# A routed matrix product with a convolution ahead of it: x gathers moved ahead, last expert choice and one block load put earlier

## The reference

```python
y = conv_general_dilated(x, cond_2048[:, None, :], ..., feature_group_count=D) + b   # 8 taps, causal
logits = einsum('bsh,eh->bse', y, w_router);  idx = argmax(logits, axis=-1)
out = x + take_along_axis(einsum('bsh,efh->bsef', y, w_experts), idx)                # one of 8 experts
```

## Time and profile before

| | us |
|---|---|
| median of 3 runs (lowest, highest) | 522.29 (520.93, 523.53) |
| the profiled execution's own time | 518.85 |
| its span, first to last instruction | 517.0 |
| TensorE busy in the span | 503.7 (97%) |
| VectorE, ScalarE, GpSimd busy | 287.8, 150.5, 134.0 |
| mean granted TensorE clock | 0.998 |

### The profile page before, as it was taken

One profiled execution on the slowest core, in us unless ns is written; L12 is line 12 of the kernel. 1 busy time (PEld: TensorE's weight loads), 2 busy tenths in 40 slices (PEclk: granted clock), 3 DMA queues, 4 the chain that ended last, 5 costly groups with the idle time before them and its releaser, 6 DMA issues.

```text
span 517.0 us, 9479 instructions
## 1 busy us (share of the span) xinstructions
PE 503.7 (97%) x2764; PEld 435.7 (84%) x2765; DVE 287.8 (56%) x418; ACT 150.5 (29%) x255; POOL 134.0 (26%) x148
## 2 busy tenths in 40 slices
PE   8999999998997999999999999999999999999995
PEld 8999999997886877888888888888888888888884
DVE  5947373769965034499773432664347244482961
ACT  2444444376001010166530100521034011340710
POOL 0003224170650112332322321213212222222312
PEclk9999999999999999999999999999999999999999
DMA  8976999997579998689999565496658855535445
GB/s 294 411 207 211 406 283 403 335 357 262 191 301 278 318 411 219 203 275 356 377 346 305 167 196 169 134 373 188 179 180 316 255 147 151 170 105 158 130 146 171
DMA packets 59623, 130.31 MB, mean 252 GB/s; under 512 B 12752, under 2 KB 32720, under 8 KB 59600
## 3 DMA queue, kind: packets, MB, share of 16 engines
q1 hardware_dynamic: 41696, 70.12, 43.7%
q0 software_dynamic: 14832, 54.27, 29.3%
q10 hardware_dynamic: 3072, 5.65, 3.4%
HBM read 94.56 MB, written 35.45 MB: 251 GB/s over the span
## 4 chain that ended last, share of the span: by engine, by line
PE 63%; issue 2%; DMA 2%; DVE 0%; DVEq 0%; POOL 0%; POOLq 0%
PE ps L851 63%; DMA x_row<-x_rows,idx 2%; DVE ys L688 0%; DMA out<-x_row,idx 0%; POOL out L930 0%; DVEq L167 0%; DVEq L701 0%; DVE x_row L698 0%; POOL idx L937 0%; DVE x_row L696 0%; DVEq L703 0%; POOLq L971 0%; DVEq L695 0%; POOLq L929 0%; POOLq L922 0%
## 5 line engine op out<-in xcount | busy, mean ns | idle before, releaser
L851 PE MATMUL ps<-w_sb,ys 128*128 128x512 f32 x1680 | 382.2, 389 | 4.2 <-DVE ys L688 3.7
L851 PEld LDWEIGHTS ps<-w_sb,ys 128*128 128x128 f32 x1680 | 314.9, 188 | 70.9 <-issue 5.1
L683 DVE STREAM_TRANSPOSE y_cols<-y_blk 128x1024 f32<-128x1024 f32 x36 | 44.8, 1244 | 147.8 <-PE ps L851 122.7
L807 PE MATMUL ps<-mats,xs 128*128 128x128 f32 x1024 | 118.3, 279 | 1.2 <-DMA xs<-x_both 1.2
L807 PEld LDWEIGHTS ps<-mats,xs 128*128 128x128 f32 x1024 | 117.3, 195 | 1.7 <-DVE mats L506 1.4
L449 ACT CAST ys<-y_cols 128x1024 fp32r<-128x1024 f32 x36 | 37.9, 1053 | 275.5 <-DVE y_cols L683 267.1
L674 DVE TENSOR_TENSOR w_sb<-w_raw,w_sb 128x1024 fp32r<-128x1024 f32 x56 | 64.2, 1220 | 3.3 <-ACT w_sb L444 3.3
L930 POOL DMA_INDIRECT out<-x_row,idx x35 | 41.1, 1175 | 83.9 <-DVE x_row L698 79.9
L937 POOL COPY idx<-ids_all 128x1 int32 (+1 forms) x36 | 15.0, 416 | 178.2 <-DMA out<-x_row,idx 115.8
L444 ACT CAST w_sb<-w_raw 128x1024 fp32r<-128x1024 f32 x56 | 56.5, 1052 | 9.4 <-PE ps L851 8.3
L918 POOL DMA_INDIRECT y_sorted<-rows,pos_i x32 | 37.0, 1157 | 75.3 <-PE ps L807 55.8
(11 more groups left out here) (102 smaller groups left out, 47.1 us busy)
## 6 DMA issues: line engine op xcount, KB each, us to landing
w_raw<-experts SPq DMA_DIRECT2D x56, 512.0 KB, 8.2
y_blk<-y_sorted SPq DMA_DIRECT2D x152, 128.0 KB
xs<-x_both SPq DMA_DIRECT2D x15, 512.0 KB
xs<-x_t SPq DMA_DIRECT2D x28, 256.0 KB
xs<-x_t ACTq DMA_DIRECT2D x20, 256.0 KB
w_first<-experts SPq DMA_DIRECT2D x8, 512.0 KB, 10.2
ids_all<-y_sorted SPq DMA_DIRECT2D x38, 1.0 KB
x_row<-x_rows,idx POOLq DMA_INDIRECT x36
```

The costliest lines, as they stand in the source:

```text
L683: V.transpose(y_cols[k][:, :, :].rearrange("p m (t i) -> p t m i", t=4), y_blk[k][:, :, :, :]).then_inc(y_blocks, 1)
L807: mm = nc.tensor.matmul(to, xs[:, n % X_RING, s % PACK, :], mats[:, s, :].rearrange("p (u n) -> p u n", n=SIDE), start=(s == sets[0]), sto ...
L851: return nc.tensor.matmul(out_ps[k][:, f * HALF:(f + 1) * HALF], ys[k][:, a, c, :], w_sb[:, c, b, f * HALF:(f + 1) * HALF], start=(c == 0 ...
```

## The change

1. `x_row` moves from the end of `w_first` to slots 4 and 5 of `xs`. GpSimd's first `look_up` now waits for the convolution of the pack that used slot 5 last (the 62nd of 64) in place of `w_split` at 8.
2. On VectorE `choose(LAST)` comes ahead of `turn_blocks` of slot 1, and `place_rows(LAST)` ahead of the last chunk's split (`low(0, 7)`) and of `low_y` of slot 1. `count_slots` goes ahead of `turn_blocks` of slot 2. The seven small steps that only the second half of the table needs leave `slot_starts`; `slot_table` is cut in two: `slot_rows` (up to `rows_ready`) runs ahead of `low_y(2)` and `residual(0)`, `slot_loads` (the seven steps and the rest) behind them.
3. On SyncE the load of slot 5 (`load_behind(FIRST - 1, ...)`) goes ahead of `load_raw(0)`.
4. At the start the first half of x's first pack is issued by ScalarE as its first transfer, and the 64 KB of factors that ScalarE issued there are issued by SyncE as its third.

```diff
-        x_row = over("x_row", [P, RING, H], raw_at + 24 * KB)
+        x_row = over("x_row", [P, RING, H], x_at + 16 * KB)
...
             load_factors(sp, 0)
-            x_0 = xs[:, 0, :, :].rearrange("p c t -> p (c t)")
-            sp.dma_start(x_0[:, 0:START_SETS * P], x_both[0][:, 0:START_SETS * P]).then_inc(x_start, 16)
             sp.dma_start(x_0[:, START_SETS * P:], x_both[0][:, START_SETS * P:]).then_inc(x_in[0], 16)
+            load_factors(sp, 1)
...
+            load_behind(FIRST - 1, RING - 1)
             load_raw(0)
-            load_behind(FIRST - 1, RING - 1)
...
         def _(act):
-            load_factors(act, 1)
+            act.dma_start(x_0[:, 0:START_SETS * P], x_both[0][:, 0:START_SETS * P]).then_inc(x_start, 16)
...
             sum_most(LAST)
             low(0, 6, w_first)
+            choose(LAST)
 
             dve.wait_ge(w_split, 4)
             turn_blocks(1, 1, 1)
-            choose(LAST)
+            place_rows(LAST)
             low(0, 7, w_first)
             low_y(1, 1)
-            place_rows(LAST)
+            count_slots()
             turn_blocks(2, 0, 2)
-            count_slots()
             slot_starts()
+            slot_rows()
             low_y(2, 0)
             residual(0, 0, 1)
-            slot_table()
+            slot_loads()
             turn_blocks(FIRST, FIRST % RING, FIRST // RING + 1)
...
-            pool.wait_ge(w_split, HC)
+            pool.wait_ge(conv_mm, pack_done(GROUPS * PACKS - X_RING + 5))
             for t in range(RING):
                 look_up(t, t, 1, t + 1)
```

More of the change, by code:

```diff
@@ L307, in load_factors @@
             queue.dma_start(factors[:, cols], factors_t[:, cols]).then_inc(factors_in[k], 16)
+        x_0 = xs[:, 0, :, :].rearrange("p c t -> p (c t)")
         @block.sync
@@ L622, in slot_starts @@
                 step(V.tensor_scalar(start, start, float(FIRST), None, ALU.add))
[L623 to L629, removed]
                 step(V.tensor_scalar(tail, count, -float(P), 0.0, ALU.add, ALU.max))
@@ L633, in slot_starts, with per_slot, slot_rows @@
                 step(V.tensor_tensor(tmp, tmp, done, ALU.add))
-            def slot_table():
-                def per_slot(a):
-                    return a.unsqueeze(1).to_broadcast([P, SLOTS, EXPERTS])
+            def per_slot(a):
+                return a.unsqueeze(1).to_broadcast([P, SLOTS, EXPERTS])
+            late, inside, val = (cmp[:, i, :, :] for i in range(3))
+            def slot_rows():
                 nths = const(C_SLOT, SLOTS).unsqueeze(2).to_broadcast([P, SLOTS, EXPERTS])
-                late, inside, val = (cmp[:, i, :, :] for i in range(3))
                 step(V.tensor_tensor(late, nths, per_slot(start), ALU.subtract))
@@ L650, in slot_table, with slot_loads @@
                 V.tensor_copy(tab_i[:, 0, :], tab[:, 0, :]).then_inc(rows_ready, 1)
+            def slot_loads():
+                step(V.scalar_tensor_tensor(out=flag, in0=n_of, scalar=0.0, in1=others, op0=ALU.is_gt, op1=ALU.mult))
+                step(V.tensor_tensor_scan(more, const(C_ONES), flag, 0.0, ALU.mult, ALU.add))
+                step(V.tensor_tensor(nth, more, others, ALU.mult))
+                step(V.tensor_scalar(sign, flag, -2.0, 1.0, ALU.mult, ALU.add))
+                step(V.tensor_tensor_scan(sign, sign, const(C_ZERO), 1.0, ALU.mult, ALU.add))
+                step(V.tensor_scalar(sign, sign, 0.5, 1.5, ALU.mult, ALU.add))
+                step(V.tensor_tensor(sign, sign, flag, ALU.mult))
                 step(V.tensor_tensor(val, inside, per_slot(nth), ALU.mult))
```

## The result

The changed kernel took 518.25 us in the median of 22 runs (514.49 to 520.96), the kernel before 521.03 us in 22 runs beside them. The ratio is 0.9935 with a 95% interval of 0.9911 to 0.9960: faster by 0.65% (3.4 us by the ratio, 2.8 us between the medians). The forecast was 516.4 us (513.2 to 519.8), a gain of 1.1% (5.9 us, counted from the 522.29 us that three runs of the kernel before had given). So it was faster as forecast and within the range, and about two fifths of the gain are missing. Of each kernel one execution was profiled; the changed one took 516.58 us (forecast 513.3), span 514.8, against 518.85, span 517.0.

A forecast was written before the change was run, and what follows sets the result against it. TensorE was busy 503.7 of 517.0 us, so only its pauses could be won. 1.5 + 2.75 + 0.99 + 0.3 = 5.5 us off 518.85 gave 513.3 profiled; median 516.7, leaned to 516.4, range 513.2 to 519.8.

The forecast's parts named there:

- The choice: Ahead of the last group's rank: choosing before slot 1's transposition gains 1.5 us, bounds 0 and 1.57.
- The gathers: Last group on GpSimd: gathers go out early, scatters start at 130.5 and land at 146.2 us, bounds 145 to 148.
- Slot 3 and slot 5: TensorE's pauses ahead of these slots go: 2.75 us (bounds 0 and 2.75) and 0.99 us (bounds 0 and 0.99).
- L1 + L2: Durations of scatter 1 and gather 3 of x; TensorE pauses ahead of slot 5 for their sum less 20.4 us.
- rival (c): Earlier weight loads slow scatter 1 and gather 3: 9.2 us pause ahead of slot 5, 526.0 us median; chance 0.15, 0.06 slower.
- The term for slot 5's edit: Issuing slot 5's rows ahead of the first weights removes the 0.99 us pause ahead of slot 5.
- The start: First convolution: x issued earlier by ScalarE gains 0.3 us, bounds 1.0 and -1.5.
- Rival (b): At the start, the second pack's factors land at 8 us: 1.4 us pause, gain 3.8 in all, 518.4 us; chance 0.08.
- behind slot 5 nothing takes such a gain back: After slot 5 TensorE pauses hardly at all, so nothing later takes the gain back while these pauses set the end.
- rival (a): Slot 3's or 5's transfers land 2 to 4 us late; with 2 us left over, median 518.7 us; chance 0.14.
- the sum: Whole kernel: choice 1.5, slot 3 2.75, slot 5 0.99 and start 0.3 us make 5.5 us.

The follow-up runs named there:

- experiment 4: Changed kernel with VectorE's order as before (choice behind slot 1's transposition, positions and row table late again): 519.16 us, ratio 0.9969 to the kernel before.
- Experiment 5: Changed kernel with slot 7's rows ahead of the second weights, plus both look_ups ahead of both gathers: 514.44 us, ratio 0.9878 to the kernel before.
- Experiment 7: Changed kernel with slot 7's rows ahead of the second weights, but x_row and GpSimd's gate as before: 520.11 us, ratio 0.9972 to the kernel before.
- experiment 3: Changed kernel with slot 5's rows behind the first weights again: 518.97 us, ratio 0.9976 to the kernel before.
- experiment 6: Changed kernel with slot 7's rows ahead of the second weights, but the start as before: 514.56 us, ratio 0.9868 to the kernel before.
- experiment 8: Changed kernel with slot 7's rows ahead of the second weights, plus 16 TensorE pauses added: 581.02 us with 14 small copies each, 556.02 us with 4.

## Why the prediction was right, and where it was not

**The choice.** Right in step and size: 1.57 us went, where 1.5 were reckoned. Without this edit the pause would now be longer than before: experiment 4 has it at 4.3 us, because GpSimd's gather now makes slot 1's rows late. The two edits hold each other up.

**The gathers.** Right, with each time 0.8 to 1.7 us late, 0.5 of it from the convolution: positions 131.2 (130.2 forecast), scatters from 132.2 (130.5), slot 3's load at 147.0 (146.2; bounds 145 to 148). The prediction named the cause, the gathers beside slot 1's rows, and covered it by the upper bound of 148. Experiment 5 measures 2 us and more on these rows and about 0.8 us on the scatters. Experiment 7 shows what the gate is worth.

**Slot 3 and slot 5.** Right: both pauses gone, slot 3's low part at 156.3 against 155.5 forecast. Gather 3 of x went out at 163.4 and was added at 171.7, so L1 + L2 of rival (c) was 6.4 + 8.4 us, far from the 20.4 at which a pause begins. The term for slot 5's edit, 0.99 us, was too small: with the others in place slot 5 pauses for 3.9 us without it, and the median is 1.9 us higher (experiment 3). A term read from one pause holds only as long as the pauses ahead of it stay.

**The start.** 0.3 us was forecast and 0.27 seen ahead of the first matmul, but the second pack's matrices were late in three traces with this start, by 1.4 to 1.6 us, where TensorE began at its fast pace, and by 0.4 in one where it began slowly. The prediction held that their factors may land as late as 6.6 us; they were in at 6.84. Rival (b) is real, and experiment 6 puts the whole edit at nothing. The 0.3 us of the sum were met by luck.

**The step that failed** is the sentence that behind slot 5 nothing takes such a gain back. It was read from the brackets of a trace in which TensorE came to slot 7 at 206.8 us. There it found rows that had been transposed 7 us ahead; this is the line of the kernel before:

```profile
199.96 1.25 DVE L683 STREAM_TRANSPOSE y_cols<-y_blk 128x1024 f32<-128x1024 f32 x1 [4.32 <-issue]
```

Now it comes 5.7 us earlier, and the rows are transposed at 199.06, hardly earlier at all, because they lie behind 8 MB of weights on one queue, the first of which was issued only 1.1 us earlier (158.08 for 159.16). The prediction counted that traffic for rival (c) and looked only at gather 3 and slot 6 in it (slot 6's rows, expected by 176, were in at 179.7, and its low part was done 3.7 us before TensorE needed it). Slot 7 takes 1.8 and 3.1 us in the two traces; with its rows ahead of the weights the gain is 1.2%, about the size that was forecast. The changed kernel itself lies in the range because its bounds had room for 2 us of pauses left over, which rival (a) expected at slot 3 or 5 and not at slot 7.

**What the sum left out** is that pauses cost more than their length. By experiment 8 a pause of slot 3's length in the kernel before (2.75 and 4.53 us in its two traces) and one of slot 7's in the changed kernel (1.78 and 3.09) carry a chance of another 1.6 us; the first trace of the kernel before drew none, and three of these four pauses had one. The pauses of 0.99 and 1.57 us are shorter than any that was priced. How much of the difference between the medians this makes is not shown.

## What to carry to other kernels

When pauses are taken from an engine that is otherwise full, it arrives earlier everywhere; go on through the later work and ask for each input how much earlier than needed it was in, and whether it moves along or is pinned by a queue. Put small transfers that are needed soon ahead of large ones that are needed late on the same queue. Price a pause of TensorE of 2 us or more as its length plus the chance of a stretch at half the clock, which was 7 in 15 here for 2.7 to 2.8 us and 10 in 10 from 3 us on.

## What the runs showed of the hardware that was not expected

Behind 12 of the 20 added pauses of 2.7 us or more (all five of over 3.6), and behind 1 of 12 of 1.85 us, TensorE's granted clock fell for a few microseconds, which cost 1.4 to 1.6 us each time. A gather of 512 KB from GpSimd's queue put beside 512 KB of row loads on SyncE's queue made these take 7.0 to 7.4 us in six traces and 9.6 in one, instead of 4.6 to 4.9 in the four without it. And the pace at which TensorE works through the first 16 matmuls was 2.05 us in some executions and 3.79 in others, with the granted clock shown as 1.00 in the one as in the other; why is open.
